# Flamingo-style two-layer kernel: z rows and inner activations kept as fp16 halves and turned by the DMA queue, and a joined query/key weight in layer 1

## What is computed

```python
# layer 0: 4 heads of 64, keys from 256 context rows (192 channels) and 256 latents
x = x + tanh(g_xattn[0]) * xattn0(ctx, x, mask)
# layer 0 experts: logits, top 2 of 8, and one shared expert for every token
h = silu(z @ W1[e].T) * (z @ W2[e].T)          # 256 -> 352
y = h @ W3[e].T                                # 352 -> 256
# layer 1: one head of 256
q = z @ Wq + bq ; k = ctx @ Wk + bk ; v = ctx @ Wv + bv
x = x + tanh(g_xattn[1]) * softmax(q @ k.T / 16) @ v
# layer 1 experts: top 1 of 8
y = gelu(z @ W1[e] + b1[e]) @ W2[e] + b2[e]    # 256 -> 512 -> 256
x = x + tanh(g_ffn[1]) * p * y
```

## Time and profile before

| | |
|---|---|
| three timed runs | 1256.54, 1256.4, 1250.9 us; median 1256.4 us |
| the profiled execution | 1255.76 us, of which the trace spans 1253.9 us |
| busy: PE, PE weight loads | 1113.0 us (89%), 859.0 us (69%) |
| busy: DVE, ACT, POOL | 765.0 us (61%), 600.4 us (48%), 412.0 us (33%) |
| mean granted TensorE clock | 0.94 |
| DMA | 116.21 MB, 93 GB/s over the span |

### The profile page before, as it was taken

One profiled execution on the slowest core, in us unless ns is written; L12 is line 12 of the kernel. 1 busy time (PEld: TensorE's weight loads), 2 busy tenths in 40 slices (PEclk: granted clock), 3 DMA queues, 4 the chain that ended last, 5 costly groups with the idle time before them and its releaser, 6 DMA issues. The chain is left out here.

```text
span 1253.9 us, 31159 instructions
## 1 busy us (share of the span) xinstructions
PE 1113.0 (89%) x8451; PEld 859.0 (69%) x8452; DVE 765.0 (61%) x2494; ACT 600.4 (48%) x1400; POOL 412.0 (33%) x485
## 2 busy tenths in 40 slices
PE   3999999999999944999999999965999998289996
PEld 2677777777777733777777777744777777256664
DVE  5467777777777662344444444434788887447775
ACT  3466665666566521444444444422555555033442
POOL 3345555556465430000000000004566662212222
PEclk9799999999999866999999999986999999579999
DMA  4123121311221112222222222225764541433341
GB/s 132 32 66 101 57 69 56 101 63 55 67 82 50 45 64 71 74 79 79 79 79 79 78 79 78 79 81 156 269 192 155 165 151 59 118 89 106 109 110 52
DMA packets 94382, 116.21 MB, mean 93 GB/s; under 512 B 12479, under 2 KB 80049, under 8 KB 94066
## 3 DMA queue, kind: packets, MB, share of 16 engines
q1 hardware_dynamic: 82594, 84.50, 22.1%
q0 software_dynamic: 10576, 29.41, 6.7%
q10 hardware_dynamic: 1152, 1.58, 0.5%
HBM read 70.43 MB, written 45.92 MB: 93 GB/s over the span
## 5 line engine op out<-in xcount | busy, mean ns | idle before, releaser
L1487 DVE TENSOR_TENSOR e_z_low<-e_z_cols,e_z_high 128x256 f16<-128x256 f32 x142 | 59.9, 422 | 209.5 <-ACT e_z_high L1431 209.2
L1431 ACT ACTIVATE e_z_high<-e_z_cols 128x256 f16<-128x256 f32 x142 | 54.5, 384 | 254.8 <-PE e_z_cols L1403 254.8
L1128 PE MATMUL a_out<-a_v_ones,a_probs 128*128 128x65 f32 x1024 | 140.6, 281 | 0.0
L1128 PEld LDWEIGHTS a_out<-a_v_ones,a_probs 128*128 128x128 f32 x1024 | 126.8, 195 | 15.3 <-issue 15.3
L464 POOL DMA_INDIRECT z_rows<-r_z_tokens,r_slot_idx x96 | 96.4, 1004 | 75.8 <-ACT r_z_tokens L455 35.7
L1608 POOL IOTA a_first_numbers<- 128x2 int32 x1 | 0.1, 125 | 367.7 <-POOLq L69 367.7
L772 ACT ACTIVATE a_probs<-a_scores,a_latent_bias,a_k_scales 128x256 f32<-128x256 f32 x128 | 65.3, 561 | 94.5 <-PE a_scores L1114 57.1
L1497 DVE TENSOR_TENSOR e_hidden_low<-e_hidden_cols,e_hidden_high 128x384 f16<-128x384 f32 (+1 forms) x142 | 83.6, 588 | 36.8 <-ACT e_hidden_high L1446 36.7
L1393 PE MATMUL e_first<-w_high,e_z_high 128*128 x412 | 96.6, 316 | 4.2 <-DVE e_z_low L1487 3.5
L1393 PE MATMUL e_first<-w_low,e_z_high 128*128 x412 | 96.3, 316 | 0.0
L1393 PE MATMUL e_first<-w_high,e_z_low 128*128 x412 | 96.3, 316 | 0.0
(11 more groups left out here) (339 smaller groups left out, 3083.3 us busy)
## 6 DMA issues: line engine op xcount, KB each, us to landing
e_z_rows<-z_rows SPq DMA_DIRECT2D x142, 128.0 KB, 2.0
y_rows<-e_y_rows SPq DMA_DIRECT2D x103, 128.0 KB, 1.7
w_stage_first<-in_w SPq DMA_DIRECT2D x18, 352.0 KB
a_ctx_in<-in_ctx SPq DMA_DIRECT2D x32, 192.0 KB, 3.7
e_token_rows<-z_rows SPq DMA_DIRECT2D x39, 129.0 KB, 2.1
residual<-in_x SPq DMA_DIRECT2D x16, 256.0 KB, 3.6
z_rows<-r_z_tokens SPq DMA_DIRECT2D x16, 256.0 KB, 2.2
a_y_shared<-y_rows SPq DMA_DIRECT2D x16, 256.0 KB, 2.8
```

What stands on the lines that cost most here:

```text
L1128: ins = pe.matmul(O[t][:, h * (D + 1):(h + 1) * (D + 1)], pm[x][:, jt, t * P:(t + 1) * P], va[p][:, jt, h, :], start=i + x == 0, stop=i + ...
L1431: act.activation(xh[p][:].rearrange("p k s -> p (k s)"), ZT[:, 0:KC * P], ACT.Copy).then_inc(zhigh, 1)
L1487: v.tensor_tensor(xl[p][:].rearrange("p k s -> p (k s)"), ZT[:, 0:KC * P], xh[p][:].rearrange("p k s -> p (k s)"), ALU.subtract).then_inc( ...
```

## The change

1. **Experts, both layers.** The rows in DRAM hold z as two fp16 halves side by side (the same 1024 bytes as 256 fp32 values). SP loads a tile's z with a DMA that transposes on the way (128 rows x 512 halves to 128 x 4 x 128), straight into what the first products read. The hidden rows are split before they are turned: ACT writes the high half and DVE the low half into `hrow` (SBUF), and SP turns both by one SBUF-to-SBUF DMA (128 x 768 or 128 x 1024 halves). PE's fp32 transposes and the splits of z in this stage are gone. The second products move from tile s-2 to tile s-3.
2. **Route.** z is one fp32 buffer; `act_z_high` (ACT) and `pool_z_low` (POOL) write its halves into the rows that are scattered or stored. `pool_z_low` stands behind `pool_scatter` in a POOL step.
3. **Weights of layer 1.** The new class `NextWeights` loads and splits them in 64 pieces of 128 x 256, one per step, in the steps 12 to 75 of experts 0. Attention 1 loads and splits none.
4. **Attention 1.** Since q·k = (z Wq + bq)·(ctx Wk + bk), Wq and Wk are multiplied once into `wqk` (256 x 193), and the scores are taken between z·`wqk` and the context itself with a column of ones. The projection of k is gone. What the left-out term adds to a row of scores is the same for all its keys, and softmax drops it.

```diff
@@ Route
-    def vector_z(self, v, n, p, x, shared):
+    def vector_z(self, v, n, x):
         v.wait_ge(self.rstd_ready, n + 1)
-        v.wait_ge(self.scattered[p], count((n - p) * (8 * self.K * T)))
+        v.wait_ge(self.z_turned, count(n))
+        v.wait_ge(self.z_low, count(n))
+    def act_z_high(self, act, n, p, shared):
+        act.wait_ge(self.scattered[p], count((n - p) * (8 * self.K * T)))
+        act.wait_ge(self.z_ready, n + 1)
+        for t in range(T):
+            ins = act.activation(self.zhalf[p][t][:, 0:C], self.z[:, t, :], ACT.Copy)
+        ins.then_inc(self.z_high, 1)
+    def pool_z_low(self, pool, n, p):
+        pool.wait_ge(self.z_high, n + 1)
+        for t in range(T):
+            ins = pool.tensor_tensor(self.zhalf[p][t][:, C:2 * C], self.z[:, t, :], self.zhalf[p][t][:, 0:C], ALU.subtract)
+        ins.then_inc(self.z_low, 1)
@@ pool_scatter
+        pool.wait_ge(self.z_low, n + 1)
@@ NextWeights
+    FIRST, PIECES, AHEAD = 12, 8 * E, 3
+    def high(self, act, i, q):
+        act.activation(high[:, ds(at, C)], self.stage[q][:], ACT.Copy, scale=WSCALE).then_inc(self.high_done, 1)
+    def low(self, v, i, q):
+        v.scalar_tensor_tensor(low[:, ds(at, C)], self.stage[q][:], WSCALE, high[:, ds(at, C)], ALU.mult, ALU.subtract).then_inc(self.low_done, 1)
@@ phase_experts, sync
                     if within(i, tiles):
-                        sp.wait_ge(turned, count(i - NZ + 1))
-                        sp.dma_start(zs[p][:], zd[ds(r, P), 0:C]).then_inc(landed[p], 16)
+                        sp.wait_ge(first_done, count(i - NZ + 1))
+                        sp.dma_start_transpose(zT[p][:], zd[ds(r, P), 0:C].bitcast(F16)).then_inc(landed[p], 16)
+                    i, p = s - 1, (q - 1) % NHT
+                    if within(i, tiles):
+                        sp.wait_ge(y_done, count(i - NHT + 1))
+                        sp.wait_ge(hlow, i + 1)
+                        sp.dma_start_transpose(hT[p][:], hrow[p][:].rearrange("p h c -> p (h c)")).then_inc(h_landed[p], 16)
...
+                    if next_piece(s, AHEAD, filling):
+                        next_weights.load(sp, s - FIRST + AHEAD, (q + AHEAD) % 4)
@@ phase_experts, scalar and vector
-                        act.activation(xh[p][:]..., ZT[:, 0:KC * P], ACT.Copy).then_inc(zhigh, 1)
-                        act.activation(hh[p][:]..., HT[p % NH][:, 0:HW], ACT.Copy).then_inc(hhigh, 1)
+                        act.activation(hrow[z][:, 0, 0:F], hs[p][:], ACT.Copy).then_inc(hhigh, 1)
+                        v.tensor_tensor(hrow[z][:, 1, 0:F], hs[p][:], hrow[z][:, 0, 0:F], ALU.subtract).then_inc(hlow, 1)
@@ phase_attn1, tensor
+                def join_weights():
+                    for k in range(KC):
+                        for h in range(KC):
+                            ins = pe.matmul(WB[:, k * (DC + 1):(k + 1) * (DC + 1)], wq[:, h, k * P:(k + 1) * P], wk[:, h, :], start=h == 0, stop=h == KC - 1)
-                            ins = pe.matmul(PJ[1][:, i * S:(i + 1) * S], wk[0:w, k, i * P:(i + 1) * P], cT[0:w, k, :], start=k == 0, stop=k == 1)
```

More of the change, by code:

```diff
@@ L1271, in ahead, with over_tiles, run @@
             self.of(1)
-def over_tiles(eng, step, n, experts=None):
-    def run(s, q):
+def over_tiles(eng, step, n, experts=None, next_weights=None):
+    def run(s, q, filling):
         if experts:
             experts.s, experts.q = s, q
-        step(s, q)
-    for s in range(-3, 8):
-        run(s, s % 4)
-    if experts:
-        experts.enter_loop(8)
-    end = 8 + (n - 3 - 8) // 4 * 4
-    with eng.Fori(8, end - 3, 4) as s:
-        for q in range(4):
-            run(s + q, q)
-    if experts:
-        experts.leave_loop()
-    for s in range(end, n + 3):
-        run(s, s % 4)
+        step(s, q, filling)
+    if next_weights:
+        first, end = next_weights.FIRST, next_weights.FIRST + next_weights.PIECES
+        loops = [(first, end - 4, True), (end, end + (n - 3 - end) // 4 * 4, False)]
+    else:
+        loops = [(8, 8 + (n - 3 - 8) // 4 * 4, False)]
+    at = -3
+    for first, end, filling in loops:
+        for s in range(at, first):
+            run(s, s % 4, True)
+        if experts:
+            experts.enter_loop(first)
+        with eng.Fori(first, end - 3, 4) as s:
+            for q in range(4):
+                run(s + q, q, filling)
+        if experts:
+            experts.leave_loop()
+        at = end
+    for s in range(at, n + 3):
+        run(s, s % 4, True)
 def phase_experts(nc, a, g, layer, out=None):
@@ L1336, in phase_experts, with next_piece @@
+        h_landed = [sem(f"h_landed{p}") for p in range(NHT)]
+        hhigh, hlow, y_done, y_out, blank = (sem(x) for x in ("hhigh", "hlow", "y_done", "y_out", "blank"))
         tokens_landed = [sem(f"tokens_landed{p}") for p in range(NZ)]
         biased, y_biased, slot_step = sem("biased"), sem("y_biased"), sem("slot_step")
+        next_weights = NextWeights(nc, g, a, c) if layer == 0 else None
+        FIRST, AHEAD = NextWeights.FIRST, NextWeights.AHEAD
+        def next_piece(s, ahead, filling):
+            return layer == 0 and filling and within(s - FIRST + ahead, NextWeights.PIECES)
@@ L1510, in step @@
                         v.scalar_tensor_tensor(ys[y][:], yb[p][:], token[:, SCALE - TOKEN:SCALE - TOKEN + 1], token[:, 0:C], ALU.mult, ALU.add).then_inc(y_out, 1)
-                over_tiles(v, step, tiles, experts)
+                    if layer == 1:
+                        experts.ahead()
+                    if next_piece(s, 0, filling):
+                        next_weights.low(v, s - FIRST, q)
+                over_tiles(v, step, tiles, experts, next_weights)
 def gather(pool, idx, k, t, rows, dst, done):
@@ L1595, in step @@
                         load_ctx(n + 3, 1 - q)
-                    if within(n + 3, weights.parts):
-                        weights.load(sp, n + 3, 1 - q)
                 over_batches(sp, -4, step, B - 5)
@@ L1697, in step @@
                         copy_v(n + 1, 1 - q)
-                        bias_q_or_k(n + 1, 1 - q, 1)
-                    if not early and within(n + 1, weights.parts):
-                        weights.high(act, n + 1, 1 - q)
                 over_batches(act, -1, step)
```

363 lines of the change are left out of this document (189 added, 174 removed).

## The result

| | before | after |
|---|---|---|
| median of four runs | 1255.8 us | 1419.2 us (1413.7 to 1424.3) |
| span of the profiled execution | 1253.9 us | 1415.9 us |
| experts 0, first product to last second product | 484.5 to 837.5: 353 us | 485.7 to 951.0: 465 us |
| attention 1, from there to the first product of experts 1 | 264.8 us | 261.9 us |
| experts 1, first product to last | 1102.3 to 1246.6: 144 us | 1212.9 to 1408.5: 196 us |

The ratio is 1.132 (95% interval 1.128 to 1.136): slower by 13%, where 6% faster was predicted. Both attention stages did what was forecast. All of the loss is in the two expert stages, +112 and +51 us.

The account below looks back on a forecast made before the run. PE was taken to set the pace in the experts and attention 1, with POOL nearly full there. Experts 0 -53, experts 1 -26, attention 1 -3, attention 0 +1 sum to -81 us on 1255.8: 1175 us, range 1138 to 1250.

Parts of the forecast that it names:

- SP's queue: Experts 0: two transposing DMAs, a store and often a load take 1.3 us at 0.33 us each; decides from about 0.9.
- rival 4: Experts: hidden rows late or SP's queue held 0.9 to 1.1 us per transposing DMA; about 1253 us, chance 0.05.
- PE's share: Experts 0: PE loses 0.54 us of transposes a tile, to 2.78 us; 103 tiles give 55.6 us.
- The DMA engines: Experts: 1.87 us a tile in experts 0, 2.2 in experts 1 at the plain rate; turned bytes under twice that cost.
- rival 2: Experts: turned bytes cost a bit over twice plain, tiles 3.05 and 3.1 us; 1216 us, chance 0.22.
- Rival 3: Experts: turned bytes cost three times plain or more, so the kernel is slower; 1353 us, chance 0.13.
- Latency: Experts 0: hidden rows wanted about 8.3 us later, a load lands in 2.0 us; 6 us would still do.
- Attention 1: POOL's two added operations make the period 13.05 us, +4 us, against 7 us gained at the ends: -3 us.
- Rival 1: Attention 1: POOL's addition is hidden and the cycle could shrink towards PE's 10.3 us; 1140 us, chance 0.10.
- Attention 0: `act_z_high` puts about 0.75 us ahead of the q halves, hidden with 0.5 us to spare: +1 us (0 to 12).
- The signs to look for: Profile after: experts 0 tiles 2.8 us apart, DMA share 0.6 to 0.8; share 0.95 or PE waiting shows rivals 2 to 4.

Follow-up runs that it names:

- the version with pairs and four tiles of slack: Kernel after with two tiles' hidden rows per transposing DMA, second products four tiles behind, plain DMAs on POOL's queue, row numbers fetched ahead: 1203.1 us, ratio 0.961.
- the relieved kernel: Kernel after with plain DMAs on POOL's queue, row numbers ahead, two tiles' hidden rows per transposing DMA, second products four tiles behind: 1203.1 us.
- the version with pairs: Kernel after with plain DMAs on POOL's queue, row numbers ahead and two tiles' hidden rows per transposing DMA, second products three tiles behind: 1342.9 us.

## Why the prediction was wrong, point by point

**SP's queue, the step that failed.** The prediction said: "It now issues two transposing DMAs, a store and often a load. No row shows what a transposing one holds the queue for; at 0.33 us each the four take 1.3 us. The other end is open; it decides from about 0.9 us each." The measured term is 4.6 us a tile in the filling steps: 2 x 1.21 for the turns, 0.78 for the others, 1.4 for the gaps. It was wrong in three ways. The value taken was the cheapest end of a price that no row showed. The sum counted only the DMAs, not the fetch of the row number and the addresses, which are as long again (1.5 against 1.5 us in the run with plain DMAs) and stood in the trace of before. And the queue's own decision point, 0.9 us, was given 0.05 and a time near that of before, though the real price lies beyond that point. It is the mechanism of rival 4. At 1.21 us each and without the gaps the sum would have been 2.42 + 0.78 = 3.2 us, still under the 3.32 of before; with the gaps it is 4.6: slower. So the price alone would have taken most of the gain away, and the gaps left out of the sum turned it into a loss. In experts 1 the queue was not summed at all; there it took 4.99 us a tile against 3.53.

**PE's share.** Right: 2.78 us a tile once nothing stands in the way, as the version with pairs and four tiles of slack shows. ACT, the busier of ACT and DVE there, takes 0.56 x 2.78 = 1.55 us of a tile, under the 2 us forecast.

**The DMA engines.** "I take less than twice": right, 1.45 to 1.8 by the estimate above. In experts 0 of the kernel after they play no part; in experts 1 of the relieved kernel, at a share of 0.95, half the bytes bring the tile from 3.13 us (the 3.1 of rival 2) to 2.74, but through SP's queue, which the large transfers held longer. Rival 3 (three times the plain price) has a time near the measured one, 1353 us, but the wrong mechanism: half the bytes changed 1.5%. The Trainium skill (DMA: Bandwidth & Descriptors, Latency and other measured facts) gives 261 GB/s for a transposing DMA whose pieces are not contiguous. The marginal prices above, which are estimates, are 160 KB in 0.75 us, 218 GB/s, and 192 KB in 1.19, 165 GB/s, less than that. The Trainium skill (VectorE: DVE Perf Modes, The three transpose paths) has 1309 ns for one block of 128 x 128. Here six such blocks landed 2.6 us after their issue, so that figure is not one to be multiplied by blocks; the prediction had taken it for the latency of a single one, and rightly did not multiply.

**Latency.** "6 us would still do" was never tested in the kernel after, where rows started late. In the version with pairs a landing of 4.2 us was too much with three tiles of slack. The prediction's 8.3 us counted neither the wait for the pair's second tile nor SP's queue.

**Attention 1.** Forecast -3 us, with a period of 13.05 us, 0.3 more than the 12.75 of one batch before; measured -2.9 us, and over ten batches 12.88 us against 12.63 before (first scatters at 905.55 and 1031.84 us), 0.25 more. The reading of POOL's rows held, including the 1.03 us ahead of the first gather, which is there unchanged. Rival 1 would not have come true with the addition off POOL either: the run with it on DVE gave 2 us, not 35.

**Attention 0.** Forecast +1 us; the first product of experts 0 starts 1.2 us later, which fits. It proves little: in the experiments, whose attention 0 is that of the kernel after in all but one, the same start lies anywhere from 482.4 to 490.8 us.

**The signs to look for.** "PE waiting there for the landing of hidden columns" was named as a sign of rivals 2 to 4, and it is what the trace shows; the DMA share of 0.48 told at once that it was not 2 or 3. The range, 1138 to 1250 us, left out rival 3 as it said, and also the middle of rival 4 (1253 us), of which it spoke only as a far edge.

## What to carry to other kernels

Before a change gives an issuing queue more to do, write out the queue's cycle as you would an engine's: every issue, every register fetch and every address computation between them, from the gaps in the trace. Where no row shows the price of a new kind of instruction, and the sum has a point from which it decides, the chance belongs to that point, not to the cheap end. And when the queue has been relieved, look in the new trace for what it now consists of: here a fetch ahead, four numbers in one fetch and a larger transfer each kept part of their price in the same queue, and the pairs lost until they had one more tile of slack.

## What the runs showed of the hardware

- A transposing DMA held SP's queue 1.17 to 1.24 us (medians of whole runs) whether it carried half of z, z, or half or all of a tile's hidden rows; a plain one 0.33 to 0.48 us. For two tiles' hidden rows it was 1.41 us in experts 0 (384 KB); in experts 1 (512 KB) it was 1.6 us at a DMA share of 0.66 and 2.0 at 0.95. Fewer and larger ones relieve the queue, until size or load eats it up.
- Fetching a number from SBUF into a register of SP and using it costs 0.6 us where nothing tests it, 0.8 to 1.1 us with a test of its bounds. The fetch itself is 0.27 us for one number and 1.13 for four at once, so that four in one fetch made the mean cycle only 0.14 us a tile shorter.
- The landing of a transposing DMA for a tile's hidden rows rose as the DMA engines became busier in experts 0: 2.5 us at a share of 0.48, 2.8 at 0.68, 3.4 at 0.80 and 3.5 at 0.89. That of a pair was 4.2 us at 0.65 and 3.8 at 0.89, so there the load is not what decides.
- A plain DMA issued from POOL took 0.54 to 0.55 us of it, from SP 0.33 to 0.48 and from ACT 0.35. When POOL's queue issued the last store of a stage, the next stage's first load was issued 5.9 us after it, in one kernel 9.3; with SP's queue 2.3.
